# A two-layer attention network on one core: the first attention's outputs go out by DMA and are divided late, and its opening gets other fillers and a shorter first lot on GpSimd

## What is computed

```python
s = einsum('bhqd,bhkd->bhqk', q, k) / sqrt(8)
p = exp(s - max_k s)
out = (p @ v) / sum_k p          # [2, 16, 1024, 8], not causal
```

## Time and profile before

| | us |
|---|---|
| median of 3 runs | 1898.36 |
| lowest and highest | 1895.8 and 1913.83 |
| the profiled execution | 1908.71 |
| its span in the trace | 1906.9 |

### The profile page before, as it was taken

How to read it: one execution, slowest core, us unless ns; L and a number is a source line. 1 busy time by engine, 2 the same in 40 slices (tenths; PEclk the granted TensorE clock), 3 DMA queues, 4 the chain that set the end, 5 groups by cost and what they waited for, 6 DMA issues and landing times. The chain is left out here.

```text
span 1906.9 us, 45876 instructions
## 1 busy us (share of the span) xinstructions
PE 1637.0 (86%) x17422; PEld 865.1 (45%) x17422; DVE 1480.8 (78%) x1734; ACT 1348.1 (71%) x2668; POOL 882.1 (46%) x526
## 2 busy tenths in 40 slices
PE   6889999999787677766777769989999999899996
PEld 2325555555444444433444433334565555344442
DVE  3788999998299999999999965447888844566456
ACT  4418888888799999989999953434777763654443
POOL 0175666665199999999999971000000002000000
PEclk8859999999998988899888989996999998999998
DMA  3343444443598888988888841121312100000000
GB/s 129 126 169 140 155 158 160 162 151 124 190 320 307 318 306 304 303 278 304 303 317 293 299 158 45 39 45 44 45 38 46 29 3 18 0 1 0 0 6 17
DMA packets 82504, 278.86 MB, mean 146 GB/s; under 512 B 11159, under 2 KB 11954, under 8 KB 81311
## 3 DMA queue, kind: packets, MB, share of 16 engines
q1 hardware_dynamic: 68223, 225.67, 35.7%
q0 software_dynamic: 13824, 50.34, 6.8%
q10 hardware_dynamic: 288, 0.45, 0.1%
HBM read 214.72 MB, written 61.21 MB: 145 GB/s over the span
## 5 line engine op out<-in xcount | busy, mean ns | idle before, releaser
L1700 POOL TENSOR_TENSOR hc<-st,ct 128x1024 f32<-128x1024 f32 x256 | 596.4, 2369 | 13.7 <-DVE st L1646 12.7
L1646 DVE TENSOR_TENSOR_SCAN st<-da,banks 128x1024 f32<-128x1024 f32 x256 | 562.7, 2266 | 16.3 <-ACT da L1603 5.5
L528 ACT ACTIVATE attn_probs<-banks 128x512 f32<-128x512 f32 (+3 forms) x640 | 324.9, 534 | 94.1 <-PE banks L362 77.1
L362 PE MATMUL banks<-attn_qa,attn_ka 75*32 75x512 bf16 (+3 forms) x3584 | 348.0, 365 | 9.2 <-DMA attn_qa<-attn_mrow 3.0
L581 DVE TENSOR_REDUCE attn_mx<-banks 128x1 f32<-128x1024 f32 x256 | 309.9, 1223 | 31.3 <-PE banks L362 19.3
L1611 ACT ACTIVATE ut<-b_turned,mats 128x128 f32<-128x128 f32 x1024 | 311.8, 388 | 1.7
L362 PE MATMUL banks<-attn_ka,attn_qa 72*32 72x512 bf16 (+3 forms) x3584 | 290.9, 380 | 17.5 <-DVE attn_mx L578 10.4
L1603 ACT ACTIVATE da<-dt,mats 128x1024 f32<-128x1024 f32 x256 | 282.6, 1139 | 26.1 <-DVE st L1646 21.3
L1528 PE MATMUL banks<-hc,onecols 128*32 128x512 f32 x1024 | 155.6, 684 | 95.8 <-POOL hc L1700 73.3
L766 POOL TENSOR_TENSOR made_ahead<-b_turned,x_turned 128x1024 f32<-128x1024 f32 x96 | 183.9, 1915 | 92.1 <-DVE attn_mparts L595 69.3
L578 DVE CUSTOM_DVE_ANT_0 banks<-banks,attn_maskwide 128x128 f32<-128x128 f32 (+7 forms) x256 | 191.2, 775 | 33.9 <-PE banks L362 30.7
(11 more groups left out here) (447 smaller groups left out, 1943.6 us busy)
## 6 DMA issues: line engine op xcount, KB each, us to landing
dt<-dt_rows SPq DMA_DIRECT2D x256, 512.0 KB, 5.6
ahead<-made_ahead POOLq DMA_DIRECT2D x96, 512.0 KB, 3.6
ua<-ahead SPq DMA_DIRECT2D x96, 512.0 KB, 6.0
attn_qa<-q_lin SPq DMA_DIRECT2D x144, 64.0 KB
attn_ka<-k_lin SPq DMA_DIRECT2D x72, 64.0 KB
moe_w<-in_moe_w SPq DMA_DIRECT2D x2, 2048.0 KB, 10.1
mats<-in_mats SPq DMA_DIRECT2D x1, 2988.5 KB, 13.1
xparts_kept<-xparts_lin SPq DMA_DIRECT2D x3, 512.0 KB, 7.9
```

The lines of the kernel that those rows point to most:

```text
L362: last = nc.tensor.matmul(out[sl(t, 32), :], lhs[:, sl(t, 32)], rhs, start=start, stop=True, skip_group_check=True)
L528: nc.scalar.activation(probs[s % 4][:, jj, c0:BLK], scores_exp[jj][:, c0:BLK], ACT.Exp, scale=scale).then_inc(probs_ready, 1)
L1646: nc.vector.tensor_tensor_scan(st[n % 4][:, :], da[n % 4][:, :], pair[:, :, :].rearrange("p h t -> p (h t)"), 0.0, ALU.mult, ALU.add).then ...
L1700: nc.gpsimd.tensor_tensor(hc[n % 8][:, :], st[n % 4][:, :], ct[:, b * SEQ:(b + 1) * SEQ], ALU.mult)\
```

## The change

For the first attention alone (`by_rows = not causal`):

- V carries 8 columns of ones, so a half unit's bank holds per head 8 rows of numerators and 8 equal rows of sums. There are two tiles `osb`, one per half.
- `turn_out`, `out_norm`, the final turn (L503) and ACT's final copies (L563) are gone. SP sends each half unit out with 8 DMAs of 8 x 512 float32 (`out_rows`): the numerators to `attn_t`, the sums to `ssm_in`, both feature-major.
- DVE divides late, a block of 128 x 512 at a time (`divide`: reciprocal in place, then a multiplication): batch 0's two blocks at s = 12 and 13 of the last unit, the third at s = 23, the fourth at the very end. The last half's four DMAs of sums are issued by ACT.
- The scan's loads stand ahead of the last `out_rows`, and the wait for them behind it.
- In the opening the bf16 fillers are gone; behind n = 16, 17 and 18 stands one float32 matmul of 128 x 128 by 512 on real data (`warm_filler`).
- POOL's first lot is 5 products instead of 7.

```diff
-        osb = k.sb(f"{tag}_osb", [128, BLK], F32, ctx)
+        osb = [k.sb(f"{tag}_osb{i}", [128, BLK], F32, ctx) for i in range(1 if causal else 2)]
+        by_rows = not causal
+        den_t = tok
...
+                def out_rows(i, qb):
+                    g, b = units[i]
+                    cols = slice(b * SEQ + qb * BLK, b * SEQ + (qb + 1) * BLK)
+                    sp.wait_ge(osb_ready, 2 * i + qb + 1)
+                    for j in range(4):
+                        heads = sl(4 * g + j, HD)
+                        sp.dma_start(attn_t[heads, cols], osb[qb][32 * j:32 * j + HD, :]).then_inc(out_sent[qb], 16)
+                        if i == UNITS - 1 and qb == 1:
+                            continue
+                        sp.dma_start(den_t[heads, cols], osb[qb][32 * j + HD:32 * j + 2 * HD, :])\
+                            .then_inc(out_sent[qb], 16)
...
                 for i in range(UNITS):
+                    if i > 0 and by_rows:
+                        out_rows(i - 1, 1)
                     rows(i, 1)
                     if i + 2 < UNITS:
                         load_part(i + 2, 0)
+                    if by_rows:
+                        out_rows(i, 0)
...
                 front.sync_third(sp)
+                if by_rows:
+                    out_rows(UNITS - 1, 1)
+                front.sync_last(sp)
...
-                        if s == OUT_AT and i > 0:
+                        if s == OUT_AT and i > 0 and not by_rows:
                             turn_out(i - 1, 1)
-                        if s == MID + 3:
+                        if s == MID + 3 and not by_rows:
                             turn_out(i, 0)
...
+                def warm_filler(bank, n):
+                    nc.tensor.matmul(bank[:, 0:n], k.m("W1", n=128), k.x[:, 0:n], start=True, stop=True)
...
-                    if n >= (own_from - 6 if causal else 8):
+                    if causal and n >= own_from - 6:
                         filler(scores_exp[0][:, :])
+                    if not causal and first_half <= n < first_half + 3:
+                        warm_filler(scores_exp[0], BLK)
...
+                def divide(b, qb):
+                    unit = max(i for i, u in enumerate(units) if u[1] == b)
+                    blk = 2 * b + qb
+                    num, den = attn_t[:, sl(blk)], den_t[:, sl(blk)]
+                    last = unit == UNITS - 1 and qb == 1
+                    if last:
+                        dve.wait_ge(out_sent[1], 128 * unit)
+                        dve.wait_ge(den_last, 64)
...
+                    link(nc.vector.reciprocal(den, den), taken[0], inverted)
...
+                    nc.vector.tensor_tensor(num, num, den, ALU.mult)
...
-                    if n >= 7 and n % 6 == 1:
-                        pool.wait_ge(self.mparts_ready[(n // 6 - 1) % 2], (n // 6 + 1) // 2)
+                    if n >= 5 and n % 6 == 5:
+                        pool.wait_ge(self.mparts_ready[n // 6 % 2], n // 12 + 1)
```

More of the change, by code:

```diff
@@ L251, in attention @@
         own_norm = k.sem(f"{tag}_own_norm")
+        out_sent = [k.sem(f"{tag}_out_sent{i}") for i in range(2)]
+        den_last = k.sem(f"{tag}_den_last")
+        inverted = k.sem(f"{tag}_inverted")
         final_turned = k.sem(f"{tag}_final_turned")
@@ L381, in turn_max @@
                     pe.wait_ge(mparts_ready[half], i + 1)
-                    if i > 0:
-                        pe.wait_ge(normed, 2 * i - 1 + (half if not causal else 0))
-                    if causal and half == 1:
+                    if i > 0 and not by_rows:
+                        pe.wait_ge(normed, 2 * i - 1)
+                    if half == 1:
                         pe.wait_ge(mrow_ready[0], i + 1)
+                    elif by_rows and i > 0:
+                        pe.wait_ge(mrow_ready[1], i)
                     for t in range(4):
@@ L440, in turn_out @@
                     elif i + 1 < UNITS:
-                        pe.wait_ge(mrow_ready[1 if causal else 0], i + 2)
+                        pe.wait_ge(mrow_ready[1], i + 2)
                     for t in range(4):
-                        last = quad(turned[:, sl(t, TILE)], osb[:, sl(t, TILE)], k.m("ident"))
+                        last = quad(turned[:, sl(t, TILE)], osb[0][:, sl(t, TILE)], k.m("ident"))
                     last.then_inc(oturned, 1)
@@ L495, in _ @@
                     pv_quad(UNITS - 1, NE - 2, vst[1], part)
-                turn_out(UNITS - 1, 1)
-                pe.wait_ge(normed, 16)
-                for n in range(NBLK):
+                if not by_rows:
+                    turn_out(UNITS - 1, 1)
+                    pe.wait_ge(normed, 16)
+                for n in range(NBLK if not by_rows else 0):
                     if n >= 2:
@@ L560, in _ @@
                 out_copy(UNITS - 1, 1)
-                for n in range(NBLK if not residual else 0):
-                    act.wait_ge(final_turned, n + 1)
-                    nc.scalar.copy(attn_t[:, sl(n)], k.bank[n % 2][:, :]).then_inc(final_copied, 1)
+                if by_rows:
+                    g, b = units[UNITS - 1]
+                    act.wait_ge(osb_ready, 2 * UNITS)
+                    for j in range(4):
+                        act.dma_start(den_t[sl(4 * g + j, HD), b * SEQ + BLK:b * SEQ + SEQ],
+                                      osb[1][32 * j + HD:32 * j + 2 * HD, :]).then_inc(den_last, 16)
             @block.vector
@@ L610, in out_norm @@
                         .then_inc(normed, 1)
+                def divide(b, qb):
[6 more added lines that the diff above has]
+                        dve.wait_ge(den_last, 64)
+                    else:
+                        dve.wait_ge(out_sent[qb], 128 * (unit + 1))
+                    taken[0] += 1
+                    link(nc.vector.reciprocal(den, den), taken[0], inverted)
+                    if last:
+                        dve.wait_ge(out_sent[1], 128 * unit + 64)
+                    nc.vector.tensor_tensor(num, num, den, ALU.mult)
+                taken = [0]
+                last_b = units[UNITS - 1][1]
                 def body(i):
@@ L620, in body @@
                                 combine(i + 1, 0)
-                        if s == OUT_AT and i > 0:
+                        if s == OUT_AT and i > 0 and not by_rows:
                             out_norm(i - 1, 1)
-                        if s == MID + 3:
+                        if s == MID + 3 and not by_rows:
                             out_norm(i, 0)
+                        if by_rows and i == UNITS - 1 and s in (12, 13):
+                            divide(1 - last_b, s - 12)
+                        if by_rows and i == UNITS - 1 and s == MID + 7:
+                            divide(last_b, 0)
                 front.vector_first(dve)
@@ L634, in _ @@
                     body(i)
-                out_norm(UNITS - 1, 1)
+                if by_rows:
+                    divide(last_b, 1)
+                else:
+                    out_norm(UNITS - 1, 1)
                 for n in range(NBLK if residual else 0):
@@ L1837, in sync_third, with sync_last @@
     def sync_third(self, sp):
+        pass
+    def sync_last(self, sp):
         pass
```

10 lines of the change are left out of this document (7 added, 3 removed).

## The result

| | before | changed |
|---|---|---|
| median of 12 runs, us | 1900.72 | 1886.95 |
| lowest and highest | 1895.8 and 1913.83 | 1885.1 and 1890.44 |
| ratio, with its 95% interval | | 0.9929 [0.9915, 0.9943] |
| profiled execution | 1908.71 | 1886.04 |

The change is worth 13.8 us (10.8 to 16.2 by the interval); 15.35 were forecast. The two profiled executions lie 22.7 us apart, since the one of before was 8 us above its own median; so the stages have to be compared one by one.

The account below looks back on a forecast made before the run. PE was taken to bound the first attention's units, 44.77 us busy of 45.70. Turned outputs -13.05, first exponentials -1.2, clock -3.4 and end +2.3 sum to -15.35 us: 1898.36 to 1883.0 on the median, range 1875 to 1901.

Parts of the forecast that it names:

- Turned outputs: First attention's loop: fifteen turned outputs leave PE, each worth 0.87 us, 13.05 us gained, bounds 12.8 and 13.4.
- costs the DMAs and the shifted lots at nothing: 128 new output DMAs on SP and ACT, 0.61 us each: taken as 0, range 0 to +1 us per unit.
- First exponentials: Opening of the first attention: sooner combine, then fillers ahead of the turn; -1.2 us, bounds -0.8 and -1.6.
- the two fillers ahead of the turn: Opening: two float32 fillers of 1.71 us and two score blocks of 0.85 put the turn at 127.7, not 128.45.
- The clock: Opening: float32 fillers may lift PE's clock from 0.50; -3.4 us taken as the middle of 0 and -6.7.
- the clock is kept: Rival for the opening: fillers lift the clock and first slots hold it, -6.7 instead of -3.4, 1879.7 us; chance 0.25.
- The fall at 1304.2 in the earlier trace: Second attention before: clock lost again, PE busy 1.99 of 3.20 us; cited against the clock being kept.
- The slower side: Rival: clock stays low longer in unit 0, about 1900 for the first half, 1920 for all 32 slots; chance 0.10.
- The end: From the last ACT copy to the scan: 8.9 us against 6.6, so +2.3 us, bounds -1.6 and +5.
- The reciprocal: Last 128 x 512 reciprocal at the end: 3.35 us if cost is per element, 0.77 if per instruction; 3.35 taken.
- the estimate worked out from it, 4.3 us: Reciprocal at the end by the skill's repeat count of 8: 4.3 us, making the end +3.2 instead of +2.3.
- The fillers without effect: Rival for the opening: fillers change nothing about the clock, opening gives only -1.2, time 1886.4 us; chance 0.15.

Follow-up runs that it names:

- experiment 1: The changed kernel with the opening of before (identity fillers from n = 8, first lot of 7): 1897.13 us, ratio 0.9981 of before.
- experiment 4: The changed kernel with POOL's first lot of 7 products again instead of 5: 1894.03 us, ratio 0.9965 of before.
- experiment 2: The kernel before with the new opening alone (three float32 fillers, first lot of 5): 1897.98 us, ratio 0.9977 of before.
- experiment 5: The changed kernel with the last of GpSimd's 96 products not waiting for the last combine: 1885.17 us, ratio 0.9928 of before.
- experiment 8: The changed kernel with the turn of a second half's maxima one place earlier, ahead of the slot's second exponentials: 1890.27 us, ratio 0.9948 of before.
- experiment 3: The changed kernel without any filler in the first opening, lot of 5 kept: 1892.43 us, ratio 0.9952 of before.
- experiment 9: The changed kernel with the bf16 identity fillers of before in place of the three float32 ones, lot of 5 kept: 1892.35 us, ratio 0.9949 of before.
- experiment 12: The changed kernel with the last product not waiting, the last half's sums sent first, and the first maxima's turn ahead of all fillers: 1884.85 us, 0.9925 of before.

## Why the prediction was right, step by step

The time, 1883.0 forecast and 1886.95 measured, came out right with two of its terms off in opposite ways: the loop gave 3.1 us less than its term and the clock 2.8 more. That these two nearly cancel is luck. The first exponentials gave 0.65 less and the end cost 2.35 more, which makes the stages' 12.1 instead of 15.35.

- **Turned outputs, 13.05 forecast.** The mechanism held: each of the fifteen gave its 0.87 us, PE stayed the bound, DVE came to 40.5 (40.4 forecast). But 10.0 us came (10.3 in the loop, -0.3 in the last half unit). The step that failed is the one that takes the whole 13.05 as a gain and costs the DMAs and the shifted lots at nothing: new waits of PE took 3.4 us back, and shorter ones gave 0.4. SP itself kept up: most issues took 0.62 to 0.69 us (single ones up to 1.73), and the three row DMAs went out 0.03 us behind ACT's copy in every unit. In a second half PE starts 3.52 us behind their first issue (326.98 to 330.50) where it was 3.37 (341.25 to 344.62). This comes with the new loop and not with the lots: the weight load's wait there is 0.58 to 0.69 us in experiments 1 and 4, which have the new loop and a first lot of 7, and 0.42 to 0.50 in experiment 2, which has the old loop and a lot of 5. The same holds for the wait at 397. The last unit's 1.1 is the last product's DMA (experiment 5), a cost of the shifted lots that the forecast did not see; experiments 1 and 4 do not have it. What in the new loop lengthens the landing is open, and experiment 8 does not tell.
- **First exponentials, -1.2 forecast.** -0.55 came (1.67 less the 1.12 won earlier). The combine was as worked out, and so was the stretch behind the turn, 4.7 us, though its end was the row DMAs and not the last filler. The term that was mis-sized is the two fillers ahead of the turn: each held PE for 2.0 us (122.16 to 124.16) where 1.71 was taken, and a score block for 0.98 instead of 0.85, so the two pairs took 5.96 us instead of 5.12.
- **The clock, -3.4 forecast between 0 and -6.7.** It was kept: 6.2 us came in this pair of traces. This is the rival "the clock is kept". The fall at 1304.2 in the earlier trace rows was a bad guide. Experiments 1, 3 and 9, without the float32 fillers, have 0.50 for 8.6 to 16.3 us behind the first exponentials, and experiment 2, with them in the old loop, has 1.00: fillers of this kind lift the clock. Experiment 4 suggests, by one trace, that the lot has to go with them.
- **The slower side**, a clock that stays low for longer, shows in no trace of the changed kernel. Its runs lie 5 us apart, those of before 18; but the runs of experiment 1, with the old opening, lie only 6 apart, and those of experiment 2, with the new one, 12.6, so the smaller spread is not shown to be the opening's doing.
- **The end, +2.3 forecast.** +2.8 came up to the scan's first DMA, and 1.8 more within the scan's first steps, which the sum did not follow; other traces with the same end show 0.0 to 1.9 there. The reciprocal was exact, 3.35 us; ACT's issues were 0.91 us instead of 0.61. The Trainium skill, page VectorE: DVE Perf Modes, in its walkthrough, gives a repeat count of 8, and the estimate worked out from it, 4.3 us, is too high by the measurement.
- **The fillers without effect.** This rival fell: in experiment 9 PE was busy 16.23 of 16.30 us at 0.50, with the old fillers, and in the changed kernel the clock rose. The Trainium skill, page TensorE: Matmul & The Clock Gate, Part 1, has sustained matmul activity release the throttle; with activity read as PE's busy time, experiment 9 does not agree.

## What to carry to other kernels

A step that leaves the engine that sets the pace is worth its own time minus what its replacement does to the waits of that engine; look for whose DMAs land between an issue and the instruction that waits for it. Where an engine's clock depends on what ran before, a filler counts by its kind, and another engine's pacing (here GpSimd's first lot) may decide whether it works, by one trace. In a chain at the end of a stage, send first what the longest step waits for, and check the first steps of the next stage before counting a gain there. Where stages without an edit differ by 9 us from one execution to the next, read what a change is worth from its own stages.

## What the runs showed of the hardware that was not expected

- A DMA issue of 8 x 512 float32 mostly took 0.62 to 0.69 us on SP (up to 1.73) and 0.91 on ACT.
- TensorE's clock rose at 128.8 within the third float32 filler (128.52, changed kernel) and at 127.7 within the second (126.27, experiment 12); in experiment 4, with a pause of 0.67 us ahead of the third filler, it stayed at 0.50 to 149.8, in one trace. With bf16 fillers PE was busy 25.31 of 27.70 us and 16.23 of 16.30 us at 0.50 (experiment 9).
